# Expert rings of four half rounds in place of two, in a mixture-of-experts decoder layer

## The reference

```python
x = layernorm(x + attention(x))                    # 16 heads of 16, four sequences of 512 rows, D = 256
x = layernorm(x + cross_attention(x, ctx))         # bidirectional attention with a context, then W_qv
probs = sigmoid(x @ router_w.T + expert_bias)      # 2048 tokens, 160 experts
top_w, top_idx = top_k(probs, 8)
top_w = top_w / (sum(top_w) + 1e-9) * 2.5
routed = sum over the 8 chosen e of top_w[e] * (silu(x @ w_gate[e].T) @ w_down[e].T)   # inner size 128
shared = silu(x @ w_gate_shared.T) @ w_down_shared.T
x = layernorm(x + routed + shared)
```

## Time and profile before

| | us |
|---|---|
| median of 3 runs | 1308.21 (1307.52 to 1311.49) |
| the profiled execution's own time | 1307.05 |
| its span | 1305.2 |
| PE busy | 877.0 (67%) |
| DVE busy | 531.2 (41%) |
| ACT busy | 431.1 (33%) |
| POOL busy | 365.5 (28%) |
| mean granted TensorE clock | 0.824 of full speed |

### The profile page before, as it was taken

One profiled execution on the slowest core, in us unless ns is written; L12 is line 12 of the kernel. 1 busy time (PEld: TensorE's weight loads), 2 busy tenths in 40 slices (PEclk: granted clock), 3 DMA queues, 4 the chain that ended last, 5 costly groups with the idle time before them and its releaser, 6 DMA issues. The chain is left out here.

```text
span 1305.2 us, 18288 instructions
## 1 busy us (share of the span) xinstructions
PE 877.0 (67%) x4146; PEld 598.9 (46%) x4146; DVE 531.2 (41%) x1412; ACT 431.1 (33%) x958; POOL 365.5 (28%) x369
## 2 busy tenths in 40 slices
PE   8459999999588834925730067667676676776492
PEld 4324444444356622713520055556565565665371
DVE  2156667763225733624636022223222222222187
ACT  4305666567234222123100033333333333333211
POOL 4000000000000072170172735454454444455200
PEclk9858999999789876866865578788888888888697
DMA  7999999996210131120031467878777877787592
GB/s 216 263 220 274 292 270 267 280 295 223 69 39 27 65 123 47 48 112 34 23 126 52 178 191 218 240 224 264 232 242 235 243 228 216 229 239 239 172 422 108
DMA packets 125687, 244.26 MB, mean 187 GB/s; under 512 B 28599, under 2 KB 68705, under 8 KB 117232
## 3 DMA queue, kind: packets, MB, share of 16 engines
q1 hardware_dynamic: 106352, 206.50, 53.1%
q0 software_dynamic: 17184, 35.20, 7.4%
q10 hardware_dynamic: 2112, 2.10, 0.5%
HBM read 147.34 MB, written 108.66 MB: 196 GB/s over the span
## 5 line engine op out<-in xcount | busy, mean ns | idle before, releaser
L1454 POOL DMA_INDIRECT contributions<-e_y,e_dest x230 | 223.8, 973 | 260.2 <-ACT e_y L1441 176.8
L1374 PE MATMUL e_psg<-e_xt,e_w 128*128 128x128 f32 x920 | 176.4, 323 | 122.2 <-DVE e_xt L1420 83.5
L1374 PEld LDWEIGHTS e_psg<-e_xt,e_w 128*128 128x128 f32 x920 | 148.1, 229 | 137.5 <-DVE e_xt L1420 92.8
L1586 POOL DMA_INDIRECT row_pool<-rows,places x128 | 126.6, 989 | 285.3 <-issue 158.9
L446 DVE TENSOR_REDUCE a_mx<-a_psS 128x2 f32<-128x1024 f32 x128 | 152.1, 1219 | 100.4 <-PE a_psS L331 98.8
L1420 DVE COPY e_xt<-e_psx 128x256 f32<-128x256 f32 x230 | 97.0, 423 | 209.1 <-PE e_psx L1363 136.6
L1383 PE MATMUL e_psy<-e_w,e_g 128*128 128x256 f32 x460 | 162.8, 441 | 16.0 <-ACT e_g L1434 9.9
L423 ACT ACTIVATE a_e<-a_psT 128x512 f32<-128x512 f32 x256 | 131.3, 605 | 81.4 <-PE a_psT L353 81.4
L1434 ACT ACTIVATE e_g<-e_psg 128x128 f32<-128x128 f32 x230 | 63.8, 277 | 223.9 <-PE e_psg L1374 125.4
L1441 ACT ACTIVATE e_y<-e_psy,e_weight 128x256 f32<-128x256 f32 x230 | 109.0, 474 | 83.0 <-PE e_psy L1383 55.0
L1363 PE MATMUL e_psx<-c_ident,e_x 128*128 128x128 f32 x460 | 99.7, 303 | 45.0 <-DMA e_x<-row_pool 44.6
(11 more groups left out here) (217 smaller groups left out, 1002.2 us busy)
## 6 DMA issues: line engine op xcount, KB each, us to landing
e_w<-w SPq DMA_DIRECT2D x230, 256.0 KB
row_pool<-fill SPq DMA_DIRECT2D x32, 1260.0 KB, 8.6
e_x<-row_pool SPq DMA_DIRECT2D x230, 140.0 KB
c_c<-contributions SPq DMA_DIRECT2D x16, 1024.0 KB, 13.4
a_k<-k_parts SPq DMA_DIRECT2D x32, 256.0 KB
v_heads<-p_v SPq DMA_DIRECT2D x4, 1024.0 KB, 6.9
a_q<-q_parts SPq DMA_DIRECT2D x16, 256.0 KB
a_q<-q_parts SPq DMA_DIRECT2D x32, 128.0 KB
```

The costliest lines, as they stand in the source:

```text
L1374: last = nc.tensor.matmul(psG[:, f.k % 2, 0:n], W[:, f.slot, c * INTER:(c + 1) * INTER], XT[:, f.k % 2, c * n:(c + 1) * n], start=c == 0, ...
L1454: nc.gpsimd.indirect_dma_start(out=contrib, out_offset=bass.IndirectOffsetOnAxis(ap=dest[:, page(f) + k:page(f) + k + 1], axis=0), in_=Y[: ...
L1586: nc.gpsimd.indirect_dma_start(out=pool, out_offset=bass.IndirectOffsetOnAxis(ap=place[:, b % 2, t, k:k + 1], axis=0), in_=rows[:, b % 2, ...
```

## The change

`HALVES` goes from 2 to 4. A round has 20 entries, and `W`, `X`, `Y`, `e_weight`, `e_dest` and the semaphores of the loads and scatters have 20 (or 4, by halves) in place of 10 (or 2). `BODIES`, the greatest number of rounds, goes from 32 to 16, so the loop is 15 long. The places of the weights are now in two tiles: the ten that mix fills ahead, as before, and ten more that exist only in `experts`. In the first round SP therefore also issues the weight loads of entries 10 to 19, each behind its row load and without a wait. The number of rounds is now the quotient by 12, or by 8, rounded up.

```diff
-HALVES = 2
+HALVES = 4
+FETCHED = 2 * ENTRIES
 RING_E = HALVES * ENTRIES
 PAGES_E = HALVES * SLOTS
-BODIES = 32
+BODIES = 16
...
-            for h in range(HALVES):
+            for h in range(FETCHED // ENTRIES):
                 listed = tables.half(h)
                 for j in range(ENTRIES):
                     tables.load_weights(sp, w, h * ENTRIES + j, listed[COLUMN[j]])
...
-                    do(nc.vector.tensor_scalar(last_i[:, 0:1], last_i[:, 0:1], 10, None, ALU.arith_shift_right))
-                    do(nc.vector.tensor_scalar(last_i[:, 1:2], last_i[:, 1:2], 9, None, ALU.arith_shift_right))
+                    do(nc.vector.tensor_scalar(last_i[:, 0:1], last_i[:, 0:1], 11, None, ALU.arith_shift_right))
+                    do(nc.vector.tensor_scalar(last_i[:, 1:2], last_i[:, 1:2], 10, None, ALU.arith_shift_right))
...
-        self.W = sb("e_w", [P, RING_E, DC * INTER + D], F32)
+        self.fetched = sb("e_w_first", [P, FETCHED, DC * INTER + D], F32)
+        self.later = None
...
+    def weights(self, slot):
+        return self.fetched[:, slot] if slot < FETCHED else self.later[:, slot - FETCHED]
+
...
+        tables.later = sb("e_w", [P, RING_E - FETCHED, DC * INTER + D])
...
                     load_rows(at, v)
+                    if at.n >= FETCHED:
+                        tables.load_weights(sp, w, at.slot, v)
                     return
```

More of the change, by code:

```diff
@@ L1264, in half @@
             max_val=EXPERTS, skip_runtime_bounds_check_because="every entry is an expert's number or the shared expert's")[1]
+    def weights(self, slot):
+        return self.fetched[:, slot] if slot < FETCHED else self.later[:, slot - FETCHED]
     def load_weights(self, sp, w, slot, e):
-        return sp.dma_start(self.W[:, slot], w[bass.ds(e, 1)].rearrange("a p n -> (a p) n")).then_inc(self.w_in[slot], 16)
+        return sp.dma_start(self.weights(slot), w[bass.ds(e, 1)].rearrange("a p n -> (a p) n")).then_inc(self.w_in[slot], 16)
 def experts(nc, tokens, tables, last_sent, w, pool, contrib):
@@ L1289, in experts @@
         ident, ident_in = tokens.ident, tokens.ident_in
-        W, w_in = tables.W, tables.w_in
+        W, w_in = tables.weights, tables.w_in
+        tables.later = sb("e_w", [P, RING_E - FETCHED, DC * INTER + D])
         X, Y = sb("e_x", [P, PAGES_E, ROW]), sb("e_y", [P, PAGES_E, D])
@@ L1373, in step @@
                     for c in range(DC):
-                        last = nc.tensor.matmul(psG[:, f.k % 2, 0:n], W[:, f.slot, c * INTER:(c + 1) * INTER],
+                        last = nc.tensor.matmul(psG[:, f.k % 2, 0:n], W(f.slot)[:, c * INTER:(c + 1) * INTER],
                                                 XT[:, f.k % 2, c * n:(c + 1) * n], start=c == 0, stop=c == DC - 1)
@@ L1383, in step @@
                         last = nc.tensor.matmul(psY[:, f.k % 2, k * D:(k + 1) * D], G[:, f.k % 2, k * P:(k + 1) * P],
-                                                W[:, f.slot, DC * INTER:], start=True, stop=True)
+                                                W(f.slot)[:, DC * INTER:], start=True, stop=True)
                     last.then_inc(downed, 1)
```

## The result

| | before | after |
|---|---|---|
| median of 9 runs each, us | 1309.86 (1303.12 to 1314.53) | 1318.85 (1316.36 to 1325.57) |
| the profiled execution's own time, us | 1307.05 | 1322.47 |
| its span, us | 1305.2 | 1320.3 |
| mean granted TensorE clock | 0.824 | 0.826 |

The ratio of after to before is 1.0078, with a 95% interval of 1.0051 to 1.0106: the change makes the kernel slower by 10.2 us (6.7 to 13.9); the two medians lie 9.0 us apart. The two profiled executions lie 15.4 us apart, because the one of before is 2.8 us under its median and the one of after 3.6 us over. What follows keeps these 6.4 us in mind.

What follows compares the result with a forecast made beforehand. SP's instruction stream was taken to pace `experts`; +12.0 (ten entries) + 5.3 (slow steps) - 6.6 (edges) - 4.4 (skipped passes) = +6.3 us, from the 1308.2 median 1314.5, predicted as 1314, range 1292 to 1328.

Steps and rivals of the forecast that it cites:

- The pace: Loop of `experts`: SP's own instruction stream sets the pace, 2.05 us for an entry, with the ring never full.
- the count of entries: Rounds of `experts`: twelve rounds of 20, 240 entries, ten more than before and all padding; 220 in the loop.
- rival 2: SP's loop edges: code fetched again at each of 11 edges, +8 to +41 us, 1322 to 1355; chance 0.06.
- rival 3: Loop of `experts`: the deeper ring evens out bursts and thins slow steps, 1285 or 1303, far case 1225; chance 0.25.
- The 0.53 us for an entry: SP's loop: share of each entry's 2.05 us put down to slow steps; ten more entries +5.3 us.
- The ring itself at nothing: Ring of 20 in `experts`: SP waits only 0.2 us now, so 0; POOL's last check 0.1 us.
- The ten cheap entries and their slow steps: First round on SP: ten more entries without waits at 1.2 us each, +12.0, and their slow steps, +5.3.
- Skipped passes: PE at the loop's end: four skipped passes in place of nine, 0.88 us each, on the path, -4.4 us.
- The prediction's sign: End of `experts`: SP's last issue to combine's first load some 18 us in place of 22.2 would confirm skipped passes.
- Loop edges: SP's loop: 11 fewer edges at 0.6 us each, -6.6 us, with bounds -5.5 and -8.0.
- Rival 1: Loop of `experts`: the DMA engines set the pace, not SP; +12.9 us, 1321, or +16, 1324; chance 0.18.
- Rival 4: Number of rounds: does not come out as 12; with 13, +41 us; chance 0.01.

Runs made afterwards that it cites:

- series two: Follow-up runs on another chip (kernel before 1288.8 us); the changed kernel, run again unchanged against the kernel before, took 1294.37 us, ratio 1.0046.
- The shorter loop: Kernel before with a loop of 23 passes in place of 31, so one skipped pass in place of nine: 1106.34 us, ratio 0.9959.
- series one: First follow-up runs, on a chip where the kernel before took 1111.5 us and no profile shows slow steps; the changed kernel was not run in it.

## Why the prediction was right, and which term was off

The forecast was 1314 us, 6.3 us above the kernel before. The measured time is 1318.85, and the kernel is slower by 10.2 us (6.7 to 13.9) in the first comparison and by 5.9 (2.5 to 9.5) in series two. The pace and the count of entries were right. That the number came out as near as it did is in part luck, as terms that were off by up to 6 us cancelled.

*The pace.* Right. SP never waits for the ring, before or after; more instructions on SP lengthen the loop by their own duration, fewer shorten the kernel by 3%, and a third of the bytes taken away changes nothing.

*One reading was wrong.* The 3.7 us without an issue in the earlier trace rows are not one long halt. They span a loop edge and the reading of the table: the same stretch takes 1.97 us on the chip without slow steps (808.36 to 810.33 above), so 1.8 us are slow steps. The upper price of rival 2 and the bunches of rival 3 rested on the 3.7. The 0.53 us for an entry didn't; it agrees with 2.05 less the 1.52 without scatters.

*The ring itself at nothing.* Right as far as the runs can tell, but for the DRAIN. SP has no wait that more places could take away. With SP relieved, where it does wait, 20 places are no faster than ten once the padding is paid. POOL's DRAIN is 2.5 us longer, 1.6 of them with the places, where the prediction had 0.1 for the end of POOL. No pair of runs compares the two depths with the same number of entries.

*The ten cheap entries and their slow steps, +12.0 and +5.3.* Right in kind, 3 us too large: 17.3 was the sum, and the profile shows 14.9 us from the 11th to the 21st row load, or 14.2 without the 0.7 of the step onto the loop, which has only moved. The second profile of the same kernel has 14.3, or 13.6.

*Skipped passes, -4.4.* Right in kind, somewhat small: PE's idle time between the loop and its last two steps is 2.33 us in place of 7.29, which is -5.0, and from the last row load to the last scatter it is -5.9. The shorter loop gave 0.58 for a pass by times, which would be -2.9. The prediction's sign, some 18 us from SP's last issue to combine's first load, came out as 19.2 (1231.78 to 1251.0), since the DRAIN gave back 2.5.

*Loop edges, -6.6.* This is the term that was mis-sized most. The price of an edge in the short body was nearly right (0.49 measured, 0.6 taken), but the term took it that a body of 20 has the same edge and nothing else. Measured on the chip without slow steps, the long body gives back all but 0.07 us of it at its own edge and at two places inside it, so the term is -0.8 (-1.8 by the means). On the chips with slow steps no run isolates it.

*Combine, at nothing.* It is 1.5 us shorter in the profile. Why isn't shown.

The sum with the measured terms, 14.2 - 0.8 - 5.9 + 2.5 - 1.5, is +8.5, and the runs show +10.2 (6.7 to 13.9) and +5.9 (2.5 to 9.5). It takes the edges from another chip. The two profiled executions themselves have +4.8 in the loop where it has -0.8, and the 6.4 us by which they stray from their medians are as much as that gap.

*The loop in the two profiles.* The prediction set 2.02 us for an entry as its test, and called itself wrong beyond 0.05 of it. The profile of after shows 2.073 (454.0 / 219), a hair outside; the second profile of the same kernel has 2.01, inside. One profile isn't fine enough to judge a term of 0.03 us an entry.

*Rival 1* named 1321 us, nearer to 1318.85 than the forecast of 1314. The time alone would have favoured it. The halved weight loads exclude it on a chip with slow steps: by it they should have saved a good part of the 20 points of DMA time that they freed. On the chip of series one the DMA engines are nearly full too, at 0.97 busy. What the Trainium skill says under "DMA: Bandwidth & Descriptors", section "Issuing engines are not separate DMA queues", that issuing is usually small beside the DMA itself, doesn't hold here: two issues, their waits and their registers take 1.32 us and more, and the 0.406 MB that they ask for take 1.30 at 313 GB/s. Taking one of the two off SP is worth 2.6 to 3.2%.

*Rival 2*, code fetched anew at each edge, fell. The instruction queues from 785 to 1231 us of the changed kernel:

```profile
q8 instruction: 2, 0.03, 0.0%
q14 instruction: 3, 0.02, 0.0%
```

All five packets come before 820 us, in SP's first pass through the loop. From 820 to 1231 us, in which every engine runs its later passes, the DMA queues are these two alone:

```profile
q1 hardware_dynamic: 57884, 81.55, 69.0%
q0 software_dynamic: 9697, 14.16, 9.5%
```

The 0.12 us steps inside the long body are not explained by this. For attend's loop the prediction read the earlier trace rows too well: the queues shown there are those of 190 to 264 us, and from 187 to 245, its second pass, there is one packet of 8 KB, at 189 us.

*Rival 3*, that depth helps, fell with the ring: the time is above both its 1285 and its 1303. *Rival 4* fell with the count of 240.

## What to carry to other kernels

Before a ring is made deeper, look at whether its producer waits for it: a wait that takes 17 ns at the median and has no row in the view of waits says that the next place has always been free, and that depth isn't what is lacking. Whether the producer's own instruction stream or the transfers are the pace is the next question; here the rows landed within 3.3 us of their issue, and halving the bytes of the weights settled it. Then take instructions off that stream (here one of two DMA issues, -3%), and price what a longer round brings with it: padding to a whole round cost a full entry's time for each empty entry, and a loop body of twice the length saved almost nothing at its edges.

## What the hardware showed that was not expected

The slow steps cost more than anything that was changed here. On three chips they are in the loop in every profile of a kernel that makes its scatters, and hold instructions of SP that wait for nothing for up to some 0.7 us at a time. On the one chip where it was tried they went with the scatters, which made the kernel 112 us faster, and stayed when the scatters wrote nothing.

On a fourth chip no profile shows any, and the kernel before takes 1111.5 us there in place of 1287 to 1310. The other indirect DMAs of the program, POOL's 128 scatters into `row_pool` in mix, show where the rest of that difference lies. First the shorter-loop kernel on the fourth chip, then the kernel before:

```profile
L1586 POOL DMA_INDIRECT row_pool<-rows,places x128: 967/972/1574, 455.7 to 655.8; - x128
```

```profile
L1586 POOL DMA_INDIRECT row_pool<-rows,places x128: 967/973/1817, 457.0 to 746.9; - x128
```

Until the first scatter the two are 1.3 us apart. From the first to the last it is 200 us in place of 290, and from the first row load of `experts` to the last 344 in place of 457. So nearly all of the difference between the chips lies after POOL's first indirect DMA; that mix has the same slow steps isn't shown.

A loop body of 20 entries on SP was slower by 0.12 us at two of its places, each time at the same ones, and POOL's DRAIN at the end took 0.88, 1.70 or 3.33 us by the number of places and entries. No row explains either.
